# Reordering the work inside one step of a hand-scheduled graph-attention layer

## The reference, cut to what matters

```python
h = relu(layernorm(x)); x = x + GNN(h, adj)          # deg*(h Wi + b) + adj @ (h Wj)
h = relu(layernorm(x)); x = x + GAT(h, adj)
# GAT, for each of 8 batches, N = 1024 tokens, F = 256:
e = leaky_relu(f1[:, None] + f2[None, :], 0.01)      # 4 heads in layer 1, 1 in layer 2
attn = softmax(where(adj > 0, e, -1e9))
out  = elu(attn @ (h W))                             # layer 1's four heads feed layer 2
y    = relu(out w1 + b1) w2 + b2 + out               # after layer 2, then a layer norm
```

## Time and profile before

| what | value |
|---|---|
| median of 3 runs | 1734.39 us |
| the profiled execution | 1733.93 us |
| its span in the trace | 1732.2 us |
| TensorE matmul busy | 1582.8 us (91%) |
| VectorE busy | 1450.6 us (84%) |
| ScalarE busy | 1377.8 us (80%) |
| GpSimd busy | 1021.5 us (59%) |
| mean granted TensorE clock | 0.974 of full speed |

### The profile page before, as it was taken

How to read it: one execution, slowest core, us unless ns; L and a number is a source line. 1 busy time by engine, 2 the same in 40 slices (tenths; PEclk the granted TensorE clock), 3 DMA queues, 4 the chain that set the end, 5 groups by cost and what they waited for, 6 DMA issues and landing times.

```text
span 1732.2 us, 36184 instructions
## 1 busy us (share of the span) xinstructions
PE 1582.8 (91%) x13119; PEld 1319.7 (76%) x13120; DVE 1450.6 (84%) x2520; ACT 1377.8 (80%) x1858; POOL 1021.5 (59%) x1425
## 2 busy tenths in 40 slices
PE   5448989999999999999999999999999999989975
PEld 3336877788887887788787887788887887878753
DVE  5877689879999799979999799988999798998483
ACT  4177499879988698878988799878988799899560
POOL 4064367546765567656775576656776476775261
PEclk9769999999999999999999999999999999999988
DMA  8256599769996798779978799769978799798572
GB/s 261 68 134 110 98 176 161 126 95 183 184 152 111 126 188 161 123 115 166 194 135 119 117 183 179 127 103 154 208 132 123 116 161 177 123 125 141 95 111 36
DMA packets 780882, 242.45 MB, mean 140 GB/s; under 512 B 746368, under 2 KB 774016, under 8 KB 780576
## 3 DMA queue, kind: packets, MB, share of 16 engines
q1 hardware_dynamic: 771744, 231.70, 74.5%
q0 software_dynamic: 8960, 8.42, 4.2%
HBM read 38.54 MB, written 16.94 MB: 32 GB/s over the span
## 4 chain that ended last, share of the span: by engine, by line
PE 53%; DVE 13%; ACT 11%; issue 8%; DMA 7%; POOL 4%; SPq 2%; DVEq 0%; ACTq 0%; POOLq 0%
PE ps L129 9%; PE ps L1266 9%; PE ps L1260 8%; PE ps L1261 8%; PE ps L1280 5%; PE ps L138 5%; PE ps L1293 5%; DVE p_lo L1041 4%; ACT xr L918 3%; DMA pt_hi<-p_hi 3%; ACT xr L912 2%; PE ps L1341 2%; DMA cat<-f_rows 2%; DVE xr L1034 2%; SPq L809 1%
## 5 line engine op out<-in xcount | busy, mean ns | idle before, releaser
L1260 PE MATMUL ps<-pt_hi,hv_hi 128*128 128x256 f16 x2048 | 465.0, 274 | 27.5 <-DMA pt_hi<-p_hi 27.5
L1261 PE MATMUL ps<-pt_hi,hv_lo 128*128 128x256 f16 x2048 | 464.8, 274 | 0.0
L1041 DVE SCALAR_TENSOR_TENSOR p_lo<-xr,rden,p_hi 128x1024 f16<-128x1024 f32 x320 | 409.7, 1280 | 15.1 <-ACT p_hi L925 15.1
L925 ACT ACTIVATE p_hi<-xr,rden 128x1024 f16<-128x1024 f32 x320 | 365.7, 1143 | 66.3 <-POOL rden L849 66.3
L918 ACT ACTIVATE xr<-xr,shift 128x1024 f32<-128x1024 f32 x320 | 365.5, 1142 | 6.3 <-POOL shift L862 6.1
L847 POOL TENSOR_SCALAR den<-sums 128x1 f32<-128x1 f32 x320 | 184.2, 576 | 239.9 <-ACT xr L918 237.9
L860 POOL TENSOR_SCALAR zt<-mx,f1h 128x1 f32<-128x1 f32 x256 | 191.4, 748 | 226.6 <-DVE mx L1034 224.1
L1034 DVE CUSTOM_DVE_ANT_0 xr<-cat,mask_add 128x1024 f32<-128x1024 f32 x256 | 310.9, 1216 | 11.4 <-DMA cat<-f_rows 11.1
L849 POOL TENSOR_TENSOR rden<-den,minus_one 128x1 f32<-128x1 f32 x320 | 285.6, 893 | 26.7
L912 ACT ACTIVATE xr<-xr,f1h 128x1024 f32<-128x1024 f32 x256 | 292.9, 1144 | 8.2 <-DVE mx L1034 8.2
L1266 PE MATMUL ps<-pt_lo,hv_hi 128*128 128x256 f16 x2048 | 266.8, 273 | 7.4 <-DMA pt_lo<-p_lo 7.4
(11 more groups left out here) (192 smaller groups left out, 3157.7 us busy)
## 6 DMA issues: line engine op xcount, KB each, us to landing
cat<-f_rows SPq DMA_DIRECT2D x32, 512.0 KB, 4.5
out<-xx SPq DMA_DIRECT2D x32, 256.0 KB
xx<-in_x SPq DMA_DIRECT2D x28, 256.0 KB, 3.3
out<-fin POOLq DMA_DIRECT2D x28, 256.0 KB, 5.0
pt_hi<-p_hi SPq DMA_TRANSPOSE x320, 3.3
pt_lo<-p_lo SPq DMA_TRANSPOSE x320, 3.4
adj_i<-in_adj SPq DMA_DIRECT2D x4, 1024.0 KB, 11.9
f2o<-f2o_rows SPq DMA_DIRECT2D x8, 512.0 KB, 4.2
```

The lines of the kernel that those rows point to most:

```text
L925: nc.scalar.activation(p_hi[:, k % P_SLOTS, :], xr[:, k % X_SLOTS, :], ACT.Copy, scale=rden[:, k % 8:k % 8 + 1]).then_inc(hi_done, 1)
L1041: nc.vector.scalar_tensor_tensor(p_lo[:, k % P_SLOTS, :], xr[:, k % X_SLOTS, :], rden[:, k % 8:k % 8 + 1], p_hi[:, k % P_SLOTS, :], ALU.mu ...
L1260: nc.tensor.matmul(to, vh, hi, start=t == 0, stop=False)
L1261: nc.tensor.matmul(to, vl, hi, start=False, stop=False)
```

## The change

Inside one step: ScalarE takes `elu_exp` first, then `valo_high`, `rectify`, `softmax`, `high_part` (before: `softmax`, `valo_high`, `elu_exp`, `rectify`, `high_part`); VectorE takes `ht_low` behind `low_part` and `valo_low` (before: ahead of both); TensorE takes `attend` ahead of `project`. In the tables some fronts and closings move by a step or two.

```diff
-        STEADY = dict(load_x=-52, x_stats0=-47, x_stats1=-43, x_rstd=-41, x_norm0=-40, h0_high0=-40, h0_low0=-39, h0_high1=-38, h0_low1=-34,
-                      turn_h0_0=-38, turn_h0_1=-34, m0=-31, m1=-30, m2=-29, m3=-28, mj_high0=-30, mj_high1=-29, mj_high2=-28, mj_high3=-27,
+        STEADY = dict(load_x=-52, x_stats0=-47, x_stats1=-42, x_rstd=-40, x_norm0=-39, h0_high0=-39, h0_low0=-38, h0_high1=-37, h0_low1=-34,
+                      turn_h0_0=-38, turn_h0_1=-34, m0=-31, m1=-30, m2=-29, m3=-28, mj_high0=-31, mj_high1=-29, mj_high2=-28, mj_high3=-27,
...
         SECOND = dict(...
-                      hv_low1=-12, turn0=-13, turn1=-12, rows=-9, rows_out=-7, f1T=-7, f1_out=-6, save_f2=-7, load_cat=-7)
-        CLOSING = dict(ff1_0=-1, ff2_0=2, ff1_1=4, ff2_1=6, hidden_0=1, hidden_1=5, y_0=3, y_1=9, save_f2o=-20, load_f2o=-16)
-        LAST = dict(ff1_0=2, ff2_0=2, ff1_1=4, ff2_1=7, hidden_0=1, hidden_1=5, y_0=3, y_1=8, save_f2o=-13, load_f2o=-12)
+                      hv_low1=-12, turn0=-13, turn1=-12, rows=-9, rows_out=-9, f1T=-7, f1_out=-6, save_f2=-9, load_cat=-7)
+        CLOSING = dict(ff1_0=-1, ff2_0=2, ff1_1=4, ff2_1=6, hidden_0=1, hidden_1=5, y_0=4, y_1=9, save_f2o=-22, load_f2o=-16)
+        LAST = dict(ff1_0=3, ff2_0=3, ff1_1=5, ff2_1=7, hidden_0=2, hidden_1=5, y_0=4, y_1=8, save_f2o=-13, load_f2o=-12)
...
             for n in range(START, STOP):                      # ScalarE
-                if unit_at(n + 3) is not None:
-                    softmax(unit_at(n + 3))
-                j = pair_at(n - VALO_HIGH)
-                if j is not None and kinds[2 * j][0] == 1 and kinds[2 * j][2] % 8 == 6:
-                    valo_high(j)
                 for layer in (1, 2):
                     j = pair_at(n - ELU_EXP + (0 if layer == 1 else 2))
                     if j is not None and kinds[2 * j][0] == layer:
                         elu_exp(j)
+                j = pair_at(n - VALO_HIGH)
+                if j is not None and kinds[2 * j][0] == 1 and kinds[2 * j][2] % 8 == 6:
+                    valo_high(j)
                 if unit_at(n + 4) is not None:
                     rectify(unit_at(n + 4))
+                if unit_at(n + 3) is not None:
+                    softmax(unit_at(n + 3))
                 if unit_at(n + 2) is not None:
                     high_part(unit_at(n + 2))
...
                     g_low(j)                                  # VectorE
-                j = pair_at(n - HT_LOW)
-                if j is not None and kinds[2 * j][0] == 1:
-                    ht_low(j)
                 if unit_at(n + 1) is not None:
                     low_part(unit_at(n + 1))
                 j = pair_at(n - VALO_LOW)
                 if j is not None and kinds[2 * j][0] == 1 and kinds[2 * j][2] % 8 == 6:
                     valo_low(j)
+                j = pair_at(n - HT_LOW)
+                if j is not None and kinds[2 * j][0] == 1:
+                    ht_low(j)
...
             for n in range(START, STOP):                      # TensorE
+                if pair_at(n - 2) is not None:
+                    attend(pair_at(n - 2))
                 j = pair_at(n - PROJECT)
                 if j is not None and kinds[2 * j][0] == 1:
                     project(j)
-                if pair_at(n - 2) is not None:
-                    attend(pair_at(n - 2))
```

## The result

The changed kernel takes 1723.11 us (median of 7 runs, 1721.06 to 1725.09) against 1733.11 us for the kernel before on the same chip (7 runs, 1728.82 to 1736.99): a ratio of 0.994, interval 0.9929 to 0.995. That is 0.6% or 10 us less, a little more than the 0.5% under which the prediction speaks of no change, inside the range, and nearer to rival B (1723.2) than to the forecast (1727.5). The profiled execution's span is 1722.6 us, 9.6 less than before. One of the six executions of the later kernel u_dve_half took 2132 us at a granted clock of 0.746 and is left out of its ratio.

A forecast was written before the change was run, and what follows sets the result against it. TensorE's own list was taken to bound the steady part, other engines the start and end. Terms -2.1 - 2.6 + 2.2 - 1.1 - 0.8 - 2.5 = -6.9 us gave 1727.5 us from the median 1734.39; range 1721.8 to 1738.

The forecast's parts named there:

- rival B: Whole kernel: the border costs nothing and the store lets the transpose pass; -11.2 us, 1723.2 us, chance 0.30.
- TensorE's exchange: TensorE's `attend` ahead of `project`: they are issued at steps of different parity, so its list stays the same; 0 us.
- Rectify: ScalarE at the start: `rectify` fills two waits for a shift ahead of `softmax`; -2.1 us, bounds 0 and -2.3.
- the rows: Batch 1's score rows saved two steps earlier: `cat` loads earlier and VectorE waits less; -2.6 us, bounds 0 and -2.8.
- Border and y_0 in the steady part: Layer borders: `elu_exp` waits for `ht_low`, delaying `ff2_0`, +2.2 us; `y_0` later ends five TensorE waits for `g_low`, -1.1.
- `x_stats1` leaves the step ahead, so I add only 0.5: Border, one pair later: `elu_exp`'s wait of 1.28 us for `ht_low` grows only 0.5, as 3.3 us of VectorE work leaves.
- The store: Scattered store near 1548 us, two steps earlier: unit 291's transpose passes or is caught (+1.3 us); middle taken, -0.8 us.
- at most 2.85 count: Store: if the transpose passes, of 3.6 us gained at most 2.85 count, limited by the pair at 1621.
- rival E: Store: DMA queues are served by turns, so moving the store is worth nothing; 1728.3 us, chance 0.06.
- The last batch: End: `ff1_1` starts 1.2 us later, the inverse is early, `hidden_1` directly follows `ff1_1`; -2.5 us, bounds -1 and -3.5.
- Rival C: Borders: `elu_exp` held by `ht_low`, TensorE stands 23 us with D (the delay) = 6; +13.9, 1748 us, chance 0.11.
- rival D: ScalarE's work takes back early gains up to 303 us, a longer `ff1_1` wait the end's; about 1734 us, chance 0.11.

The follow-up runs named there:

- u_dve_half: Changed kernel with `ht_low` ahead of `low_part` and `valo_low` again, each scattered store but the last batch's cut into two halves; 0.9957 of the kernel before.
- u_dve: Changed kernel with VectorE's order of before (`ht_low` ahead of `low_part` and `valo_low`); ratio 0.9961 to the kernel before.
- best: Changed kernel with `ht_low` ahead as before for batches 0 to 6, last only for batch 7; median 1721.8 us, ratio 0.9938 to the kernel before.
- e_store: Kernel before with GpSimd's scattered stores alone moved two steps earlier; ratio 1.002 to the kernel before.
- e_y0: Kernel before with `y_0` alone a step later in both closing tables, and the other moves of the last batch; ratio 0.9966 to the kernel before.
- e_rows: Kernel before with batch 1's score rows alone copied and saved two steps earlier; ratio 0.9977 to the kernel before.

## Why the prediction came out as it did

**The total** came from two errors of opposite sign beside two terms that held in size. Predicted -6.9 us, profiled -9.6.

*TensorE's exchange, 0*: right; its list of matmuls, row by row, is the same before and after.

*Rectify, -2.1, and the rows, -2.6*: right, 2.06 and 2.8 us, each read from a trace in which it stood alone; in the timed runs the rows show (0.9977) and ScalarE's order doesn't (0.9997). The announced wait for `cat` of 1.7 us was 0.86.

*Border and y_0 in the steady part, +2.2 - 1.1*: the net was near, the mechanism was not. The net without the lower clock is +1.2 us, the forecast's +1.1, and that is luck: both terms were too small by about the same. `ht_low` last costs about 3.5 us and not 2.2, and `y_0` a step later gives 0.38 us in six places, 2.3 us, and not 1.1. Against the other traces with before's order in this stretch (-1.4 and -3.0) the net would be 2.6 or 4.2, too. `elu_exp` does wait for `ht_low` as announced, 20.7 us in all in 13 places (18 to 22 were given), but the delay doesn't reach `ff2_0` through `hidden_0`: TensorE has no wait of L1341 there. What fails is the step "`x_stats1` leaves the step ahead, so I add only 0.5": it went into the step of `elu`, ahead of it, and `ff1_0` behind waited 1.78, 1.79 and 0.19 us. And the step "the wait of 0.2 us for `g_low` goes" was right, but the sum lacked that `project` then waits 0.38 us for `ht_low`, 2.3 us in six periods. Against both stand 2.3 us less for `g_low` and 2.7 less for the transposes. Of the former only a part is `y_0`'s: six waits of 0.2 to 0.3 us just behind the place where `project` now waits remain in u_dve and best (1.8 us) and go where `ht_low` is last, so `project`'s wait in part only takes their place. The latter is within the scatter of the stalls. The new waits for `elu` and for `ht_low` are the announced sign of a wrong step: TensorE waits in the steady part that the rows of before don't have.

*The store, -0.8*: the mechanism was right (whether the low part of unit 291 is issued ahead of the store decides, and `ht_low` behind it makes it so), the size was not. Between "passes" and "is caught" I took the middle; the rows gave 0.7 us of shift and 0.5 us of margin, and it passed with 0.99. And "at most 2.85 count" was wrong: 6.15 us came, and 5.2 us of lead over the value ahead of the store were still there at the pair at 1621.73. Of the 6.15, 4.3 are the stall (6.31 - 1.99) and 1.9 the lower clock behind it, 3.75 us from 1560.0 to 1563.75 at 1.2 GHz, which the working never priced. Rival B had the passing, and rival E, that the store's move is worth nothing, falls: TensorE's stall ends 11.1 to 13.0 us behind the store in all thirteen traces with a whole store, also where the store is the only thing that moved (e_store). By the Trainium skill (DMA: Bandwidth & Descriptors, "Queues, rings and completion order") the engines take queues by turns. No run here shows the turns or refutes them; what fails is the step from them to a store that keeps no transpose of another queue waiting.

*The last batch, -2.5*: right in its mechanism, `ff1_1` 1.2 us later and `hidden_1` directly behind it, and right in size up to `ff2_1` (3.0 us, and 2.6 in e_y0). That the end agrees too (2.5, and 2.9 alone) is in part luck. The sum had neither the 2.0 us of lower clock that go with the wait of 5.30 us nor the longer wait for a transpose behind it, which takes most of them back.

*The lower clock behind the border stalls, not in the sum*: +2.9 us in the steady part of the changed kernel, 0 in the trace of before on which the sum was built.

Rival C, a border that costs over 17 us, and rival D, gains taken back up to 303 us, are excluded: `elu_exp` never waits over 2.2 us for `ht_low` in the changed kernel, and the lead at 333 us is 4.9 us there and 2.8 in e_rows. (The stalls that C names for D = 5.1 add up to 17.6 us, not 17.8.) Rival B's "the border costs nothing" isn't borne out: `ht_low` last costs about 3.5 us.

## What to carry to other kernels

Two parts of a change can each be worth nothing or a loss and pay only together: here an order on VectorE that costs about 3.5 us put one transpose ahead of a store that a table had moved. Such a part can be taken where it pays only (the last batch), with the old order elsewhere; here that gave the shortest span, though the timed runs don't show it to be faster. When a step is moved away from one waiter, look at who stands behind it in the step that receives it. And a stall's price is the stall plus the slower matmuls behind it. A sum of a few us built on one trace has to allow for them, and for the same program running 3 to 4 us longer in the next trace.

## What the runs showed of the hardware

**The clock behind short stalls.** In the traces of before, changed and the twelve runs there are 53 border stalls of TensorE of 2.0 to 3.5 us between 333 and 1480 us, the engine busy at 2.4 GHz on both sides. Behind or within 25 of them the granted clock fell to 1.2 GHz, for 3.4 us or 6.8 us, and with the other 28 it didn't; the shortest with it was 2.06 us, the longest without 3.34. One stall of 2.29 us, ending between 164 and 170 us in every trace, was followed by it in 6 of 14. Matmuls at the lower clock take 1.3 to 2.9 us longer each time, up to 7.9 us in one execution, more than any part of this change; how much of it is left later differs (1.6 us in the kernel before run again, where the start at 1480 us moved by 0.1 us).

**A scattered 4 KB store holds SP's transposes.** While it does, the DMA engines are not idle by the profile but move little. One window of u_dve, columns as above, with the clock, the DMA share and GB/s at the end:

```profile
1548.00:1550.00 2.00, 0.00 (x0) 0.00 (x0) 2.00 (x3) 2.00 (x4) 0.94 (x2) 1.00 1.66 26
```

The share of packets under way is high (1.66) and the rate low (26 GB/s). These packets are not the store's. By the DMA view of u_dve all of the store's packets start within 4 us of its issue at 1542.28, and from 1547 to 1549 every packet is of SP's queue, the transposes: 413 of them, with a share of 2.30. Half the elements hold them 9.2 us, more than half of the 11.1 to 13.0. Why the transposes' packets take so long then is open.
